# First two tiles' row maxima added on the matmul engine instead of by DMA, and the bulk loads moved behind the first stack

## The reference

```python
x = x + gamma * attention(q=layernorm(x), k=ctx, v=ctx)     # qk = einsum('bhdq,bhdl->bhql') * scale, softmax over l
x = x + ffn(layernorm(x), w_gate, w_up, w_down, ln_weight)  # bit_linear: int8-like rows, ternary weights
# ffn: h = silu(bit_linear(x, w_gate)) * bit_linear(x, w_up); h = rms_norm(h, ln_weight); bit_linear(h, w_down)
```

## Time and profile before

| | before |
|---|---|
| device time, median of 3 runs | 230.31 us (225.52 to 231.53) |
| device time of the profiled execution | 227.79 us |
| its span | 226.0 us |
| PE busy | 169.6 us (75%) |
| DVE busy | 148.8 us (66%) |
| ACT busy | 135.3 us (60%) |
| POOL busy | 115.8 us (51%) |
| mean granted PE clock | 0.887 of full |

### The profile page before, as it was taken

The page is one execution under the profiler, slowest core; times in us unless marked ns, Lnnn a source line. Parts: engine busy times, 40 slices in busy tenths (PEclk is TensorE's granted clock), DMA queues, the critical chain, the costliest instruction groups (busy, mean ns, idle before and its releaser), DMA issues.

```text
span 226.0 us, 4319 instructions
## 1 busy us (share of the span) xinstructions
PE 169.6 (75%) x1382; PEld 97.5 (43%) x1382; DVE 148.8 (66%) x284; ACT 135.3 (60%) x274; POOL 115.8 (51%) x290
## 2 busy tenths in 40 slices
PE   0005561787798969898998989889989988973792
PEld 0002530553375533555465556455655644522332
DVE  2304662536465964897997899799899895246283
ACT  3124252653337754868868886886876975971432
POOL 4327435330523173676786587587367448347150
PEclk9999985558569985999999999999999997997589
DMA  5765989318502162026306315422600000000000
GB/s 160 235 135 156 325 214 244 97 20 179 117 0 74 48 151 64 23 70 144 98 17 174 84 40 128 99 83 79 149 11 5 0 28 7 0 23 0 26 0 23
DMA packets 15707, 19.95 MB, mean 88 GB/s; under 512 B 2597, under 2 KB 14005, under 8 KB 14677
## 3 DMA queue, kind: packets, MB, share of 16 engines
q1 hardware_dynamic: 11397, 14.43, 25.6%
q10 hardware_dynamic: 4288, 5.24, 8.3%
HBM read 15.20 MB, written 4.19 MB: 86 GB/s over the span
## 4 chain that ended last, share of the span: by engine, by line
PE 34%; POOL 25%; DVE 12%; issue 11%; DMA 9%; ACT 6%; ACTq 2%; POOLq 0%; DVEq 0%
PE psO L465 7%; PE psA L435 6%; PE psB L449 5%; POOL hw L317 5%; DMA q_stack<-mt 3%; PE psG L538 3%; POOL hq L1020 3%; DMA k_stack<-k_scratch 3%; DVE h L855 2%; DVE mneg L763 2%; DVE gu L844 2%; ACT th L679 2%; PE psG L501 2%; PE psU L501 2%; PE psG L575 2%
## 5 line engine op out<-in xcount | busy, mean ns | idle before, releaser
L763 DVE TENSOR_REDUCE mneg<-psA 128x2 f32<-128x512 f32 x128 | 82.2, 678 | 26.8 <-PE psA L435 26.6
L608 ACT ACTIVATE probs<-psB 128x512 f32<-128x512 f32 x128 | 73.5, 596 | 26.2 <-PE psB L449 25.4
L435 PE MATMUL psA<-k_stack,q_stack 72*128 72x256 bf16 x256 | 53.8, 299 | 19.7 <-DMA k_stack<-k_scratch 19.3
L449 PE MATMUL psB<-q_stack,k_stack 75*128 75x256 bf16 x256 | 51.9, 288 | 6.6 <-DMA q_stack<-mt 4.6
L465 PE MATMUL psO<-probs,vt 128*32 128x256 f32 x512 | 37.7, 416 | 1.0 <-ACT probs L608 1.0
L435 PEld LDWEIGHTS psA<-k_stack,q_stack 72*128 72x128 bf16 x256 | 23.1, 105 | 34.7 <-issue 27.9
L449 PEld LDWEIGHTS psB<-q_stack,k_stack 75*128 75x128 bf16 x256 | 23.5, 102 | 20.9 <-DMA q_stack<-mt 5.4
L317 POOL TENSOR_TENSOR hw<-h,lnw 128x512 f32<-128x512 f32 x15 | 19.2, 1278 | 22.3 <-DVE h L855 13.3
L465 PEld LDWEIGHTS psO<-probs,vt 128*32 128x32 f32 x512 | 14.1, 115 | 15.2 <-issue 8.8
L844 DVE SCALAR_TENSOR_TENSOR gu<-th,psG 128x512 f32<-128x512 f32 x15 | 10.3, 688 | 9.9 <-ACT th L679 9.9
L679 ACT ACTIVATE th<-psG,tscale 128x512 f32<-128x512 f32 x15 | 10.3, 688 | 8.5 <-PE psG L538 8.5
(11 more groups left out here) (134 smaller groups left out, 256.3 us busy)
## 6 DMA issues: line engine op xcount, KB each, us to landing
k_stack<-k_scratch SPq DMA_DIRECT2D x21, 192.0 KB
q_stack<-q_scratch SPq DMA_DIRECT2D x21, 192.0 KB
q_scratch<-q_parts SPq DMA_DIRECT2D x24, 64.0 KB, 2.6
k_scratch<-k_parts SPq DMA_DIRECT2D x21, 64.0 KB, 2.1
w_sb<-in_L_ffn_w_gate_dram ACTq DMA_DIRECT2D x1, 1024.0 KB, 6.0
w_sb<-in_L_ffn_w_up_dram ACTq DMA_DIRECT2D x1, 1024.0 KB, 6.0
w_sb<-in_L_ffn_w_down_dram ACTq DMA_DIRECT2D x1, 1024.0 KB, 15.6
out_dram<-y_sb SPq DMA_DIRECT2D x8, 128.0 KB, 1.9
```

Source lines behind the costliest of these rows:

```text
L435: mm = pe.matmul(psA[n % A_BANKS][:, qt * L:(qt + 1) * L], q_stack[0:STACK, t % NBUF, bh, qt * P:(qt + 1) * P], k_stack[0:STACK, t % NBUF, ...
L449: mm = pe.matmul(psB[b % 2][:, lt * L:(lt + 1) * L], k_stack[:, t % NBUF, bh, lt * P:(lt + 1) * P], q_stack[:, t % NBUF, bh, :], start=Tru ...
L608: act.activation(probs[:, b % RING, :], psB[b % 2][:, :], ACT.Exp, scale=SCALE).then_inc(s_exp, 1)
L763: dve.tensor_reduce(mneg[:, k % MBUF, QT * (bh % HALF):QT * (bh % HALF + 1)], psA[n % A_BANKS][:, :].rearrange("p (q l) -> p q l", q=QT), ...
```

## The change

For the first two tiles (`SEL_TILES = 2`) the maxima no longer travel by DMA. POOL makes `sel_one` at the start (one more memset and three selects), ACT widens it to `sel`, 16 selector matrices of 48 x 128, each with ones in the three rows that belong to one unit and query half. B of these tiles runs over 72 partitions, and four small matmuls (two for each of its two key halves) of 48 partitions and 128 columns add the right row of `mt` to `psB`. So B of a unit has six matmuls in place of two there; from tile 2 on all is as before. The first B of each half waits for the copy to `mt` and no longer for a DMA; SP skips four DMAs.

The bulk loads move: ACT issues gate weights, late x, late ctx, up and down weights in one go at `ACT_BULK = -4`, once the whole first stack has landed. All steps of the weights' preparation move to later places, and six groups of twelve, in place of four, are copied by DVE.

```diff
-ACT_W, ACT_LATE = -4, 19
+ACT_BULK = -4
+SEL_TILES = 2
-ACT_WS, PE_W, DVE_W, POOL_WQ, DVE_WQ = (-8, 22, 34), (3, 26, 38), (3, 26, 38), (4, 27, 39), (8, 32, 44)
-WB = {10: 0, 12: 1, 14: 2, 17: 3, 34: 4, 36: 5, 38: 6, 40: 7, 46: 8, 48: 9, 50: 10, 52: 11}
-WB_ON_DVE = (5, 7, 9, 11)
+ACT_WS, PE_W, DVE_W, POOL_WQ, DVE_WQ = (24, 46, 56), (27, 50, 60), (27, 50, 60), (30, 55, 62), (34, 59, 67)
+WB = {36: 0, 38: 1, 40: 2, 42: 3, 61: 4, 63: 5, 65: 6, 67: 7, 69: 8, 71: 9, 73: 10, 75: 11}
+WB_ON_DVE = (1, 3, 5, 7, 9, 11)
...
+        sel_one = sb("sel_one", [PARTS * HALF * QT, HALF * QT])
+        sel = sb("sel", [PARTS * HALF * QT, HALF * QT, P], BF16)
...
# SP
-                if k is not None:
+                if k is not None and k >= 2 * SEL_TILES:
...
# PE, B of a unit
-                        pe.wait_ge(s_mrow[i // HALF], DMA * (t + 1))
+                        if t < SEL_TILES:
+                            pe.wait_ge(s_mtsb, 2 * t + i // HALF + 1)
+                        else:
+                            pe.wait_ge(s_mrow[i // HALF], DMA * (t + 1 - SEL_TILES))
+                    if b == 0:
+                        pe.wait_ge(s_sel, 2)
...
-                                       k_stack[:, t % NBUF, bh, lt * P:(lt + 1) * P],
-                                       q_stack[:, t % NBUF, bh, :], start=True, stop=True)
+                                       k_stack[0:rows, t % NBUF, bh, lt * P:(lt + 1) * P],
+                                       q_stack[0:rows, t % NBUF, bh, :], start=True, stop=(t >= SEL_TILES))
+                        for qt in range(QT if t < SEL_TILES else 0):
+                            mm = pe.matmul(psB[b % 2][:, lt * L + qt * P:lt * L + (qt + 1) * P],
+                                           sel[:, QT * (bh % HALF) + qt, :], mt[:, (2 * t + i // HALF) % 2, :],
+                                           start=False, stop=(qt == QT - 1))
...
# ACT, ahead of the loop
-            load_w(act, 0)
...
# ACT, in the loop
+                if m == 2 * FIRST + 1:
+                    act.wait_ge(s_sel, 1)
+                    act.activation(sel[:, :, :], sel_one[:, :].unsqueeze(2).to_broadcast([PARTS * HALF * QT, HALF * QT, P]),
+                                   ACT.Copy).then_inc(s_sel, 1)
-                if m == ACT_W:
+                if m == ACT_BULK:
                     act.wait_ge(s_first, 2 * PARTS * DMA)
                     act.wait_ge(s_stack[0], 2 * PARTS * DMA)
+                    load_w(act, 0)
+                    act.dma_start(x_sb[:, EARLY:T, :], x_rows[EARLY:T].rearrange("g p l -> p g l")).then_inc(s_x[EARLY], DMA)
+                    act.dma_start(c_sb[:, EARLY:T, :], ctx_rows[EARLY:T].rearrange("g p l -> p g l")).then_inc(s_c[EARLY], DMA)
                     load_w(act, 1)
                     load_w(act, 2)
...
# ACT, copy to mt
-                    if k >= 2:
-                        act.wait_ge(s_mrow[k % 2], DMA * (k // 2))
+                    if 2 <= k < 2 * SEL_TILES + 2:
+                        act.wait_ge(s_b, HALF * (k - 1))
+                    elif k >= 2:
+                        act.wait_ge(s_mrow[k % 2], DMA * (k // 2 - SEL_TILES))
```

More of the change, by code:

```diff
@@ L221, in build @@
         s_mtsb = sem("max_rows_copied")
+        s_sel = sem("selectors_made")
         s_mrow = [sem(f"max_rows_loaded{i}") for i in range(2)]
@@ L442, in _ @@
                     if i % HALF == 0:
-                        pe.wait_ge(s_mrow[i // HALF], DMA * (t + 1))
-                    if b < NBUF * BH and i == 0:
-                        pe.wait_ge(s_ones[t], DMA)
+                        if t < SEL_TILES:
[4 more added lines that the diff above has]
+                        pe.wait_ge(s_sel, 2)
+                    if i == 0 and SEL_TILES <= t < SEL_TILES + NBUF:
+                        pe.wait_ge(s_ones[t % NBUF], DMA)
                     if b >= 2:
                         pe.wait_ge(s_exp, b - 1)
+                    rows = STACK_M if t >= SEL_TILES else STACK
                     for lt in range(LT):
                         mm = pe.matmul(psB[b % 2][:, lt * L:(lt + 1) * L],
-                                       k_stack[:, t % NBUF, bh, lt * P:(lt + 1) * P],
-                                       q_stack[:, t % NBUF, bh, :], start=True, stop=True)
+                                       k_stack[0:rows, t % NBUF, bh, lt * P:(lt + 1) * P],
[4 more added lines that the diff above has]
+                                           start=False, stop=(qt == QT - 1))
                     mm.then_inc(s_b, 1)
@@ L608, in _ @@
                     act.activation(probs[:, b % RING, :], psB[b % 2][:, :], ACT.Exp, scale=SCALE).then_inc(s_exp, 1)
-                if m == ACT_W:
+                if m == 2 * FIRST + 1:
[3 more added lines that the diff above has]
+                if m == ACT_BULK:
                     act.wait_ge(s_first, 2 * PARTS * DMA)
                     act.wait_ge(s_stack[0], 2 * PARTS * DMA)
+                    load_w(act, 0)
+                    act.dma_start(x_sb[:, EARLY:T, :], x_rows[EARLY:T].rearrange("g p l -> p g l")).then_inc(s_x[EARLY], DMA)
+                    act.dma_start(c_sb[:, EARLY:T, :], ctx_rows[EARLY:T].rearrange("g p l -> p g l")).then_inc(s_c[EARLY], DMA)
                     load_w(act, 1)
                     load_w(act, 2)
-                if m == ACT_LATE:
-                    act.dma_start(x_sb[:, EARLY:T, :], x_rows[EARLY:T].rearrange("g p l -> p g l")).then_inc(s_x[EARLY], DMA)
-                    act.dma_start(c_sb[:, EARLY:T, :], ctx_rows[EARLY:T].rearrange("g p l -> p g l")).then_inc(s_c[EARLY], DMA)
                 t = tile_at(m, ACT_QK1)
@@ L908, in _ @@
             pool.memset(one_rows[:, :], 1.0).then_inc(s_rows, 1)
+            link(pool.memset(sel_one[:, :], 0.0))
+            for c in range(PARTS):
+                made = pool.affine_select(out=sel_one[:, :], in_=sel_one[:, :], compare_op=ALU.not_equal, fill=1.0,
+                                          base=-c * HALF * QT, pattern=[[-1, HALF * QT]], channel_multiplier=1)
+                if c < PARTS - 1:
+                    link(made)
+                else:
+                    made.then_inc(s_sel, 1)
             pool.memset(ones[:, :], 1.0).then_inc(s_const, 1)
```

## The result

| | before | with the change |
|---|---|---|
| device time, median | 229.55 us (225.52 to 231.53, 4 runs) | 249.73 us (245.40 to 262.39, 4 runs) |
| ratio, 95% interval | 1 | 1.0845 (1.0465 to 1.1225) |
| profiled execution, its span | 227.79, 226.0 us | 252.17, 250.4 us |
| PE busy | 169.6 us | 198.6 us |
| DVE, ACT busy | 148.8, 135.3 us | 151.2, 136.9 us |

The change makes the kernel 8.4% slower (4.7 to 12.3%), where 219.5 us was forecast. Its landmarks are read against each other, and totals come from the medians.

A forecast was written before the change was run, and what follows sets the result against it. PE was taken as the bound from about slice 16; earlier, a DMA wait before the first B and the half clock cost time. Terms 8.8 + 4.0 - 2.9 - 0.5 gave 9.4 us faster: 219.5 us, range 211 to 227.5.

The forecast's parts named there:

- the price of the selectors: Tiles 0 and 1 on PE: a unit's four products cost 0.43 us at half clock, 0.22 us at full.
- rival 4: Selectors on PE cost 0.43 us a unit also at full clock, 7 us more; 222 to 225 us; chance 0.10.
- I take 8 us at the half level: Units 16 to 32: PE spends only 8 us at half clock, so the stretch takes 26 us, not 30.0.
- Rival 3: Units 16 to 43: PE stays at half clock; held low throughout, unit 43 comes at 97 to 101; chance 0.06.
- if the clock rows show 0.50 beyond 50 us: Sign of a wrong forecast: granted clock at half level beyond 50 us; 1.0 by about 42 was expected.
- The load of 35 us: Units 16 to 32: PE's work, selectors included, totals 35 us at half clock, 17.5 at full.
- So the first B comes at about 29: Start of tile 0's B: without the maxima's DMA, first B at about 29 us, 11 us earlier.
- of a possible 0 to 2.2: First stack: gate weights no longer beside tile 0's stores; 1.5 us gained, first A at 17.8, not 19.28.
- I take 13 us, landing at 33: Tile 1's stack, issued at about 20.0 us, takes 13 us, letting A of unit 16 run at about 33.
- my bounds of 10 and 18: Tile 1's stack needs 10 us at an even share (120 GB/s), 18 us at 65 GB/s.
- 74.5: A of unit 43, the first of tile 3's landmarks: forecast at 74.5 us in place of 84.5.
- the gain of 9.4: Whole kernel: summed forecast of 9.4 us faster, from shifts up to unit 43 and later selectors.

The follow-up runs named there:

- padded kernel: Changed kernel with selector products zero-padded from 48 to 72 rows and up and down weights issued at m = 25 and 37: 225.49 us, ratio 0.977.
- the issues apart: Changed kernel with ACT issuing the up weights at m = 25 and the down weights at m = 37: 245.06 us.
- staggered kernel: Against the padded kernel, late x and ctx issued at m = 25, up weights at 33, down weights at 41: 228.80 us, ratio 1.003.

## Why the prediction was wrong

**The step that failed** is the price of the selectors: "The four selector products of a unit stream 4 x 128 columns, as many as one pair of 256: 0.43 or 0.22 us a unit." With their changes of rows they cost 1.73 - 0.86 = 0.87 and 1.08 - 0.44 = 0.64 us. Columns alone are right only for products of 72 or 128 rows, which cost 0.42 and 0.22. I had rival 4 for a higher price, but bounded it by "0.43 a unit also at the full clock"; the trace before has matmuls over 72, 75 and 128 rows and none over 64 or fewer, so it could not show the bubble. Directly, 32 units x 4 x 0.11 = 14.1 us of PE time in a stretch where PE is the bound.

**The second step**, "I take 8 us at the half level", rested on the argument that "what keeps the clock low now are gaps that the change fills". The profile called PE busy for 14.00 of 14.00 us, but with a bubble at every change: in the 1.73 us of a unit the columns stream for 1.29. The lower level lasted until 100 us. Rival 3 had that sum ("arrives at 97 to 101" for A of unit 43, with 0.06): from 42.7 and with the dearer selectors it became 110.0. The sign that I had named, "if the clock rows show 0.50 beyond 50 us", did not appear, since the rows print 1.00 there. How long the level lasted went with the changes of rows: with the loads split, the first rise came at 78.5 us with four a unit (77.6 over 64 rows) and near 46 with two or none. In the kernel with 48-row selectors on the loads of before the clock rose once at 31.0 us, fell at 34.4 and is then printed as 0.50 until 119.8, so there the level doesn't have to be read from the pace (unit 16 to 32):

```profile
42.20:86.40 44.20, 43.64 (x230) 20.37 (x230) 16.68 (x33) 15.21 (x29) 8.71 (x19) 0.50 0.32 76
```

These windows are of the padded kernel, with unit 16 at 35.1 and unit 43 at 83.25:

```profile
35.10:64.75 29.65, 26.35 (x225) 18.48 (x226) 16.38 (x34) 16.52 (x31) 10.20 (x18) 0.94 0.74 176
64.75:83.25 18.50, 16.07 (x159) 12.17 (x156) 12.99 (x24) 9.90 (x22) 5.52 (x18) 0.91 0.18 38
83.25:90.25 7.00, 6.94 (x73) 3.99 (x73) 5.70 (x10) 5.92 (x12) 3.80 (x4) 1.00 0.24 60
```

Unit 16 to 32 takes 29.7 us there against 41.9 in the kernel that differs by the padding alone. Of these 12.2, 16 x 0.45 = 7.2 are the changes themselves; by this estimate the other 5 are work done at the lower level that the padded kernel does at the upper. The load of 35 us at the lower level was right: 41.9 - 7.2 = 34.7. The 8 us were not, even with the bubbles gone. By its pace the padded kernel is at the lower level until 45.8 us, which the 0.94 leaves out, and again from 56.1 to 59.5: 14.1 us. That the changes keep the level low is what the kernels have in common, not a shown mechanism: nothing was run that has the gaps without the changes.

**Third, not seen at all:** that an engine which issues DMAs can be held in the issue. I counted 4.4 MB on ACT's queue as traffic beside the stack, and cost the issues at nothing. "So the first B comes at about 29" was then 39.7; with the issues apart it was 28.8. With padded products this was worth about 5 us of the end time. With the maxima on the DMA (the loads alone, ratio 0.998) it can't be told: that kernel wasn't run with the issues apart.

**What held.** The first A came earlier, as forecast, but at 16.1 and not 17.8: 3.2 us gained, where 1.5 "of a possible 0 to 2.2" was taken. ACT's stores of tile 0 landed in 2.0 us instead of 4.6. `sel_one` on POOL was hidden, and ACT's copy to `sel` took 1.91 us (1.90 was taken). ACT's sum over the gate weights ended at 27.2 in the padded kernel, 28.3 forecast. "I take 13 us, landing at 33": 15.7 us, at 35.1, in the padded kernel, between my bounds of 10 and 18 and 2.7 us over what I took. With no bulk beside it 10.2, so the crowd matters, though not in the measure of its bytes (16.2 us in the staggered kernel). The Trainium skill, page "DMA: Bandwidth & Descriptors", section "Issuing engines are not separate DMA queues", has the traffic of all issuers share the 16 DMA engines; the 15.7 beside 10.2 us agree.

**What was still mis-sized with the defect mended.** The padded kernel reaches unit 43 at 83.25, not 74.5: 2.1 us from the stack, 3.7 between units 16 and 32 (29.7 for 26), 3.0 between 32 and 43 (18.5 for 15.5, with the clock at 0.91 by the window). And unit 43 wasn't a clean landmark: the five units behind it took 8.9 us before, at a low clock again, and 7.0 at 1.00 here. So in place of the gain of 9.4 there was one of 5.4, 230.85 to 225.49 side by side.

## What to carry to other kernels

Where matmuls of 64 or fewer rows alternate on PE with ones of 72 or more, try padding the short ones with zeros: here the padded rows cost nothing on PE, and every crossing had cost 0.11 us at either clock. (The contraction height, the rows a matmul sums over, is what is padded, not its columns.) Price a new matmul by its neighbours and not by its columns alone. An engine that others wait for should not issue a large load while several of its earlier ones are still on their way; look in the trace for how long each issue held its engine, not only for when it lands.

## What the runs showed of the hardware

A change between matmuls over 48 or 64 rows and such over 72 costs 0.11 us, at both clock levels; between 72 and 128 rows nothing. A DMA issue of 1 MB, otherwise 0.4 to 0.8 us, held ACT for 1.7 to 4.7 us when 2.4 MB of its earlier loads had not landed, and for 9.0 to 10.6 us with 3.4 MB. The printed granted clock stood at 1.00 from 41.6 to 100 us, where 256 columns took 0.21 us, the pace of the lower level: up to the first recorded rise the rows print 1.00 where the pace is the lower level's, and the pace has to be read from the matmuls' starts. PE, called busy for 14.00 of 14.00 us with bubbles in it, still ran at the lower level. The lowest median was that of the changed kernel with 128-row selectors and the up and down weights issued apart, 223.50 us, 2.7% faster than before (1.6 to 3.8%); it isn't told apart from the one with 72 rows (1.5 to 3.2%).
